# Three of q's twelve stacking transfers issued by ACT instead of SP, in the first three iterations of a cross-attention and expert kernel

## The reference

```
x = x + xattn(layernorm(x), ctx, mask)        # q = quantised linear, k and v = float32 linears of ctx
    scores = einsum('bhnd,bhld->bhnl', q, k) / sqrt(32) + mask;  attn = softmax(scores)
    o = einsum('bhnl,bhld->bhnd', attn, v);   out = quantised linear of o
x = x + ffn(layernorm(x))                     # router, top 2 of 8 experts, silu(gate) * up @ down
```

## Time and profile before

| | |
|---|---|
| time, median of 3 runs | 1579.15 us (1578.87 to 1583.02) |
| the profiled execution's own time | 1580.35 us |
| its span | 1578.6 us |
| PE busy | 1486.5 us (94%) |
| ACT busy | 882.1 us (56%) |
| DVE busy | 893.2 us (57%) |
| POOL busy | 651.3 us (41%) |

### The profile page before, as it was taken

How to read it: one execution, slowest core, us unless ns; L and a number is a source line. 1 busy time by engine, 2 the same in 40 slices (tenths; PEclk the granted TensorE clock), 3 DMA queues, 4 the chain that set the end, 5 groups by cost and what they waited for, 6 DMA issues and landing times. The chain is left out here.

```text
span 1578.6 us, 40115 instructions
## 1 busy us (share of the span) xinstructions
PE 1486.5 (94%) x11594; PEld 1311.1 (83%) x11595; DVE 893.2 (57%) x2366; ACT 882.1 (56%) x2097; POOL 651.3 (41%) x666
## 2 busy tenths in 40 slices
PE   6999999999999999999999999982599999999896
PEld 5888888888888888888888888861599999999895
DVE  7666766667666776667666776656522222222221
ACT  3776667777777677777777677760133333333232
POOL 3233333343323333343333433325355555565453
PEclk9999999999999999999999999995699999999998
DMA  8676677776777677776777677746247776675643
GB/s 259 170 199 185 181 198 214 212 189 183 226 201 202 180 205 207 213 189 183 223 206 197 183 218 192 191 136 228 73 79 186 189 190 129 135 176 115 150 79 48
DMA packets 220123, 281.08 MB, mean 178 GB/s; under 512 B 83568, under 2 KB 164976, under 8 KB 220080
## 3 DMA queue, kind: packets, MB, share of 16 engines
q1 hardware_dynamic: 203088, 246.90, 55.7%
q0 software_dynamic: 16128, 33.30, 12.1%
q10 hardware_dynamic: 864, 0.34, 0.1%
HBM read 118.31 MB, written 66.17 MB: 117 GB/s over the span
## 5 line engine op out<-in xcount | busy, mean ns | idle before, releaser
L331 ACT ACTIVATE probs<-probs,neg_max 112x375 f32<-112x375 f32 x512 | 312.2, 610 | 195.8 <-DVE neg_max L462 190.8
L462 DVE CUSTOM_DVE_ANT_0 probs<-score,neg_mask 112x375 f32<-112x375 f32 x504 | 275.4, 547 | 236.0 <-PE score L611 230.5
L619 PE MATMUL turn<-ident,probs 112*125 112x112 f32 x1536 | 262.9, 280 | 2.7 <-ACT probs_t L318 1.3
L318 ACT ACTIVATE probs_t<-turn 125x336 f32<-125x336 f32 x512 | 225.9, 441 | 69.4 <-PE turn L619 69.0
L619 PEld LDWEIGHTS turn<-ident,probs 112*125 112x125 f32 x1536 | 225.9, 189 | 35.0 <-issue 15.6
L611 PE MATMUL score<-k_stack,q_stack 96*112 96x376 f32 x496 | 200.6, 404 | 3.6 <-DMA q_stack<-q_lo 3.1
L651 PE MATMUL proj<-ctx_hi,wk_hi 128*128 128x376 f32 x512 | 176.0, 344 | 12.5 <-DVE ctx_lo L577 12.5
L1139 DVE TENSOR_TENSOR a_lo<-a_ps,a_hi 128x384 fp32r<-128x384 f32 x63 | 35.2, 558 | 244.3 <-ACT a_hi L1114 232.8
L651 PE MATMUL proj<-ctx_lo,wk_hi 128*128 128x376 f32 x512 | 171.9, 336 | 0.0
L651 PE MATMUL proj<-ctx_hi,wk_lo 128*128 128x376 f32 x512 | 171.7, 335 | 0.0
L656 PE MATMUL proj<-wv_hi,ctx_hi 128*125 128x512 f32 x384 | 151.7, 395 | 1.0 <-DVE v L536 1.0
(11 more groups left out here) (215 smaller groups left out, 3381.6 us busy)
## 6 DMA issues: line engine op xcount, KB each, us to landing
k_stack<-k_hi SPq DMA_DIRECT2D x512, 94.0 KB, 2.4
k_stack<-k_lo SPq DMA_DIRECT2D x256, 94.0 KB, 2.6
ctx_stage<-ctx_t SPq DMA_DIRECT2D x32, 750.0 KB, 5.2
q_stack<-q_hi SPq DMA_DIRECT2D x250, 56.0 KB, 2.0
w_raw_hi<-gate_up_t SPq DMA_DIRECT2D x32, 352.0 KB, 3.1
gate_up_dram_hi<-w_raw_hi SPq DMA_DIRECT2D x32, 352.0 KB, 5.4
gate_up_dram_lo<-w_raw_hi SPq DMA_DIRECT2D x32, 352.0 KB, 5.8
gate_up_hi<-gate_up_dram_hi SPq DMA_DIRECT2D x16, 704.0 KB, 9.4
```

Of the source, the lines that this page charges most:

```text
L318: act.activation(probs_t[:, h % RING_T, :, :], turn[h % 2][0:LC, 0:LT * N].rearrange("p (l n) -> p l n", l=LT), ACT.Copy).then_inc(turned_ ...
L331: act.activation(probs[:, h % DS, :], probs[:, h % DS, :], ACT.Exp, bias=neg_max[:, par % 2, h:h + 1], scale=-1.0, accum_out=total[:, par ...
L462: dve.tensor_tensor_reduce(probs[:, h % DS, :], (last_score[h % 4] if last else score[h % 2])[0:N, 0:L], neg_mask[:, p, :], 1.0, BIG, ALU. ...
L619: mm = pe.transpose(turn[h % 2][0:LC, l * N:(l + 1) * N], probs[:, h % DS, l * LC:(l + 1) * LC], W["ident"][0:N, 0:N])
```

## The change

In iterations 0, 1 and 2 ACT issues three of q's twelve transfers: group 2 in slot 11, group 3 in slot 13, and the second copy of group 3 in slot 14, each behind the exponential of its slot. All three move parts of `q_hi`. SP skips them and issues the other nine. Bytes, semaphore counts and everything from iteration 3 on stay as they were.

```diff
+    ACT_STACKS = {11: (2, 0), 13: (3, 0), 14: (3, 1)}
...
                             for r, src in ((0, q_hi), (1, q_hi), (2, q_lo)):
+                                if not inside and it < 3 and (i, r) in ACT_STACKS.values():
+                                    continue
                                 sp.dma_start(q_st[QUARTER * r:QUARTER * r + QUARTER, q, i:H:4, :].bitcast(F32),
                                              src[rows, :, :].bitcast(F32)).then_inc(q_stacked, 16)
...
+                    if h in ACT_STACKS and has_a and has_n and not inside and it < 3:
+                        i, r = ACT_STACKS[h]
+                        need(act, q_hi_made, n + 1)
+                        need(act, scored, H * it)
+                        waited(act)
+                        act.dma_start(q_st[QUARTER * r:QUARTER * r + QUARTER, (par + 1) % 2, i:H:4, :].bitcast(F32),
+                                      q_hi[QUARTER * i:QUARTER * i + QUARTER, :, :].bitcast(F32)).then_inc(q_stacked, 16)
                     if h == 12 and has_a:
```

## The result

The changed kernel takes 1586.6 us (median of 18 runs, 1581.91 to 1593.64) against 1579.27 us for the kernel before (18 runs): a ratio of 1.0049, 95% interval 1.0034 to 1.0065. It is slower, by 7.3 us in the medians. The time lies in the predicted range and on the predicted side, but past the 0.3% within which the likeliest case put it. The profiled execution has a span of 1586.7 us, 8.1 over that of before.

The account below looks back on a forecast made before the run. PE bounds the kernel, busy 1486.5 of 1578.6 us, with 3.1 us of q waits to gain. Three boundaries at +5.99 less 2.02 given back make +3.97 us: 1583.1 against the median 1579.15, range 1578.5 to 1588.

Parts of the forecast that it names:

- the likeliest case: Whole kernel: slower by 3.97 us, to 1583.1, within 0.3%; chance 0.65 with its lower part.
- The bound: First scores of batches: PE waits 3.1 us in all for q, the most that faster stacking could give back.
- rivals 2 and 3: Batches 1 to 6: late transfers queue, +11.2 us, chance 0.22; or nothing is given back, +5.99 us, chance 0.06.
- SP's share: Iterations 0 to 2: three issues fewer on SP, so its last q transfer lands 1.93 us sooner each time.
- When ACT can issue: Slot 14: issue follows the exponential's accumulator read; with 2.0 us to landing, losses of 0.89, 1.80 and 0.30 us.
- L: Batches 1 to 3: time from ACT's last issue to landing, between 2.0 and 5.4 us, taken as 3.0.
- its sign of being wrong: ACT's last transfer: the prediction is wrong if issue to landing takes over 3.3 us.
- The row of 5.4 us: SP's queue: a k transfer issued right behind the four stores took 5.4 us, the upper end for issue to landing.
- Rival 2: Batches 1 to 3: ACT's late transfers queue behind loads and stores; +11.2 us, 1590.3; chance 0.22.
- Given back: Batches 4, 5 and 6: SP gets ahead of PE, so q waits of 2.02 us go.
- the sign "the waits at batches 4, 5 and 6 are gone": Trace of the changed kernel: no q waits left at these batches, where they were 0.98, 0.68 and 0.36 us.

Follow-up runs that it names:

- early_slots: The change with ACT's same three transfers in slots 10, 11 and 12 instead of 11, 13 and 14; ratio 0.9985 to the kernel before.
- loads_last: The change, but in iterations 0 to 2 SP issues the context's load and x behind the four split-weight stores; ratio 0.9998 to the kernel before.
- stores_held: The change, but in iterations 0 to 2 SP waits for q's transfers ahead of the four split-weight stores only; ratio 1.0049 to the kernel before.
- early_everywhere: ACT's three transfers in slots 10, 11 and 12 as against the kernel before, but in all iterations; ratio 1.0022.
- only_slot14: The change, but ACT issues only slot 14's transfer and SP issues eleven; ratio 1.0094 to the kernel before.
- loads_held: The change, but in iterations 0 to 2 SP waits for all q transfers before the context's load, x and what follows; ratio 1.004 to the kernel before.
- change_everywhere: The change's three slots in all iterations, hardware loop included, instead of the first three; ratio 1.0368 to the kernel before.

## Why the prediction was right in part and wrong in its likeliest case

- **The bound.** Right: only q's waits changed at first, and 3.1 us was all there was to gain. early_slots gave back 2.4. (The prediction's own chances for its rivals 2 and 3 add up to 0.28 and not 0.27, which changes nothing.)
- **SP's share.** Right as far as it went: SP's own last transfer was no longer what PE waits for at batches 1 to 3. What I noted only as pushing the context's load 1.93 us forward was the side that mattered.
- **When ACT can issue.** Wrong, to the change's favour. I put the issue behind the end of the exponential's accumulator read (67.22 in iteration 0, and after a delayed copy 99.44 and 131.60). The rows show it 0.09 us after the exponential's start, beside it, and slot 14's exponential 1.36 us after slot 13's as before. With L = 2.0 the three waits would have been some 0.0, 0.6 and 0.35 us (the measured ones less what L had over 2.0), and not 0.89, 1.80 and 1.37 (the prediction's 0.30 and the 1.07 of SP's lateness that it leaves out). loads_last, with L of 2.8, 2.1 and 2.1, has 0.69, 0.69 and 0.51.
- **L.** This is the step that failed: "I take L = 3.0, nearer to the lower end." It measured 3.3, 5.2 and 4.5, mean 4.3, inside the bounds of 2.0 to 5.4, but over the 3.3 that the prediction itself names as its sign of being wrong. The reason that I gave, "ACT's queue is another one, so it need not stand behind all of the stores' bytes", is what the packets and loads_last refute for the context's load. At batch 1 it is the stores that ACT's transfer stood behind, for 1.2 us (stores_held). The row of 5.4 us, a transfer behind loads and stores in one queue, was nearer than that of 2.0 us. Rival 2 had this mechanism and a price of +11.2 us at L = 5.4; it got a chance of 0.22, and it is what happened. Not by the ground that the prediction gives for it, though, a late increment of the semaphore: the transfer's own packets move late. With the mean L of 4.3 the prediction's own sum gives 2.99 + 3 x 2.3 - 2.02 = +7.9 us, near the measured 7.3, but by errors that cancel (below).
- **Given back.** Right in kind, 1.33 us of the 2.02; batch 5 kept 0.69, so the sign "the waits at batches 4, 5 and 6 are gone" came in part.
- **The clock.** Missing. I let PE's wait cost its own length; 2.5 us more came from the slower matmuls behind the two longer waits.

By its own terms: three boundaries cost 7.89 - 1.07 = 6.8 us where I had 5.99, the clock 2.5 where I had nothing, and 1.3 were given back where I had 2.02. The two errors in the first term partly cancel: the part with L = 2.0 was put at 2.99 and comes to some -0.1 (0.95 less the 1.07 of before), and L's excess was put at 3.0 and comes to 6.9. That the time still fell into the range rests in part on this, so on luck.

## What to carry to other kernels

Moving DMA issues from a saturated queue to an idle engine also moves forward what stood behind them. Look at what the first queue issues next: a small transfer that someone waits for, on another engine's queue, behind a large load of the first, lands with the load. Put it ahead by a slot, or put the load behind it; either took the loss away here. And a PE wait of some 2 us or more should be costed with the slow matmuls that may follow: 1.2 to 2.4 us each in these kernels, where they followed at all.

## What the runs showed of the hardware

- A transfer's issue on ACT runs beside the activation ahead of it (0.09 us after its start), and ACT's next instruction can be held by the 0.6 us of the issue: ACT stood idle for 0.19 us ahead of the expert weights' activation in slot 12 of early_everywhere.
- A transfer on ACT's queue can stand still while SP's queue moves. In the change 477 packets of SP's queue went in 2.6 us and none of the 144 that ACT had issued at 100.15; from 103.4 on both queues moved. The Trainium skill, "DMA: Bandwidth & Descriptors", section "Queues, rings and completion order", says that each DMA engine takes turns between the queues with work, a packet at a time. By that, ACT's packets would have been mixed in, if they were there to be taken; for those 2.6 us the trace doesn't show it. Whether their descriptors were made late or the engines took them late stays open: no run tells these apart.
- Granted clock after a wait of PE: 1.00 after 1.07 us (before) and 1.21 us (change), 0.67 over the 3.2 us after 2.22 us (only_slot14), 0.65 over 2.9 us after 2.85 us and 0.50 over 2.5 us after 3.83 us (change). In stores_held it was 0.50 over the 3.0 us after 3.30 us, and in loads_held 0.68 over the 3.0 us after 1.71 us. But 1.00 followed 2.31 us (stores_held, batch 3), 2.52 us (change_everywhere, batch 2) and 3.08 us (loads_held, slot 9). So the length of the wait alone doesn't decide. Where the clock fell, the slow matmuls cost 1.2 to 2.4 us (2.4 after the 3.30 us).
